# Decayed attention: copying the transposed weights of two heads with one instruction

## The reference, cut to what matters

```
def _L2_attn_ref(x, Wq, bq, Wk, bk, Wv, bv, Wo, bo, alpha):
    q = (x @ Wq.T + bq).reshape(B, T, H, hd)
    k = (x @ Wk.T + bk).reshape(B, T, H, hd)
    v = (x @ Wv.T + bv).reshape(B, T, H, hd)
    scores = jnp.einsum('bqhd,bkhd->bhqk', q, k) * scale
    lag = jnp.abs(idx[:, None] - idx[None, :]).astype(jnp.float32)
    scores = scores * jnp.exp(-alpha * lag * DT)
    attn = jax.nn.softmax(scores, axis=-1)
    out = jnp.einsum('bhqk,bkhd->bqhd', attn, v).reshape(B, T, D)
    return out @ Wo.T + bo
```

## Time and profile before

| what | value |
|---|---|
| median of 3 runs | 4465.07 us |
| lowest and highest run | 4442.44 and 4473.7 us |
| the profiled execution, its own time | 4474.3 us |
| its span in the trace | 4472.5 us |
| decayed attention in it | about 2574 to 3191 us |
| mean granted TensorE clock | 0.822 |

### The profile page before, as it was taken

The page is one execution under the profiler, slowest core; times in us unless marked ns, Lnnn a source line. Parts: engine busy times, 40 slices in busy tenths (PEclk is TensorE's granted clock), DMA queues, the critical chain, the costliest instruction groups (busy, mean ns, idle before and its releaser), DMA issues. The chain is left out here.

```text
span 4472.5 us, 65620 instructions
## 1 busy us (share of the span) xinstructions
PE 3023.8 (68%) x22266; PEld 2082.8 (47%) x22266; DVE 2326.8 (52%) x5222; ACT 1525.0 (34%) x2598; POOL 813.9 (18%) x800
## 2 busy tenths in 40 slices
PE   6999526999932314794346299999881537599990
PEld 4555414777720313442145145555571325476790
DVE  5555663111145463499553488888534468412443
ACT  4444112333322000000222188888531332243340
POOL 0000000000018301200134350000025564000015
PEclk9999757999956556897678599999995768699995
DMA  2000000000000022000034110000151000000471
GB/s 102 1 1 0 1 8 10 5 9 9 5 6 29 6 38 39 1 0 0 4 102 145 37 39 1 1 1 1 55 181 37 31 7 1 11 10 4 140 213 60
DMA packets 124861, 150.88 MB, mean 34 GB/s; under 512 B 50012, under 2 KB 95593, under 8 KB 124041
## 3 DMA queue, kind: packets, MB, share of 16 engines
q1 hardware_dynamic: 106584, 107.60, 8.7%
q0 software_dynamic: 18096, 41.06, 2.9%
HBM read 108.23 MB, written 40.37 MB: 33 GB/s over the span
## 5 line engine op out<-in xcount | busy, mean ns | idle before, releaser
L2183 DVE CUSTOM_DVE_ANT_0 decayed_sd<-decayed_sc,decayed_decay 128x512 f32<-128x512 f32 x512 | 331.7, 686 | 86.2 <-PE decayed_sc L2060 86.0
L2138 ACT ACTIVATE decayed_pr<-decayed_sd,decayed_shift 128x512 f32<-128x512 f32 x512 | 338.9, 713 | 49.5 <-DVE decayed_shift L2190 49.3
L668 PEld LDWEIGHTS experts_down<-experts_w,experts_h 128*128 128x128 f32 x2048 | 263.9, 192 | 107.1 <-issue 103.5
L2072 PEld LDWEIGHTS decayed_tr<-all_ident,decayed_pr 128*128 128x128 f32 x2048 | 223.5, 141 | 175.5 <-ACT decayed_pr L2138 101.7
L2072 PE MATMUL decayed_tr<-all_ident,decayed_pr 128*128 128x128 f32 x2048 | 276.9, 278 | 11.0 <-ACT decayed_pt L2145 10.8
L736 DVE SCALAR_TENSOR_TENSOR L0c_G<-experts_down,all_gate,L0c_G 128x128 f32 x256 | 85.5, 351 | 371.1 <-PE experts_down L668 371.1
L441 PE MATMUL experts_up<-experts_xt,experts_w 128*128 128x256 f32 x1140 | 272.0, 386 | 0.0
L702 ACT ACTIVATE experts_h<-experts_up,experts_w 128x512 f32<-128x512 f32 x256 | 175.9, 687 | 281.1 <-PE experts_up L657 279.7
L668 PE MATMUL experts_down<-experts_w,experts_h 128*128 128x128 f32 x2048 | 264.7, 275 | 0.0
L657 PE MATMUL experts_up<-all_XNT,experts_w 128*128 x512 | 258.7, 597 | 5.3 <-DMA experts_w<-in_L_experts 5.3
L198 PE MATMUL norm_turned<-all_ident,norm_xn 128*128 128x128 f32 x128 | 35.7, 434 | 299.6 <-DVE norm_xn L136 299.6
(11 more groups left out here) (468 smaller groups left out, 6377.1 us busy)
## 6 DMA issues: line engine op xcount, KB each, us to landing
experts_w<-in_L_experts SPq DMA_DIRECT2D x78, 384.0 KB, 3.4
experts_w<-in_L_experts SPq DMA_DIRECT2D x43, 579.0 KB, 4.0
experts_tok<-rows_in SPq DMA_DIRECT2D x121, 128.0 KB, 3.4
rows_out<-experts_y POOLq DMA_DIRECT2D x121, 128.0 KB, 3.4
rows_in<-linear_zero SPq DMA_DIRECT2D x43, 128.0 KB, 1.8
experts_w<-in_L_experts SPq DMA_DIRECT2D x8, 514.0 KB, 3.4
experts_b<-in_L_experts_b SPq DMA_DIRECT2D x43, 64.0 KB, 4.2
moe_w<-in_L_moe SPq DMA_DIRECT2D x4, 514.0 KB, 3.5
```

The source lines that it names most:

```text
L668: last = pe.matmul(down[b % 2][:, t * P:(t + 1) * P], h[:, b % 2, f, t * P:(t + 1) * P], w2, start=(f == 0 and t == 0), stop=(f == nf - 1) ...
L2072: last = pe.transpose(tr[u % TURNED][:, t * P:(t + 1) * P], pr[:, u % RING, t * P:(t + 1) * P], m.ident[:, :])
L2138: act.activation(pr[:, u % RING, :], sd[:, u % RING, :], ACT.Exp, bias=shift[:, u % RING:u % RING + 1]).then_inc(exp_ready, 1)
L2183: dve.tensor_tensor_reduce(out=sd[:, u % RING, :], in0=sc[h][:, :], in1=decay[:, qt, :], scale=1.0, scalar=-3.0e38, op0=ALU.mult, op1=ALU. ...
```

## The change

The two `tr` banks become one tensor `[P, 2, 512]`, so that one instruction can read both. `keep(g, h)` now copies heads `h` and `h + 1` at once, 1024 columns. ScalarE runs it once a quad for heads 0 and 1, VectorE once a quad for heads 2 and 3. A copy waits until both of its heads are transposed (`g * G + h + 2`). The semaphores `act_kept` and `dve_kept` count one for each quad in place of two. TensorE waits before head 0 for VectorE's copy of the quad before, and before head 2 for ScalarE's copy of heads 0 and 1; heads 1 and 3 have no wait on a copy any more. On VectorE `negate(g, 1)` stands ahead of the copy.

```diff
-        sc, tr, proj, av = s.banks("sc", G), s.banks("tr", TURNED), s.banks("proj", 1)[0], s.banks("av", 1)[0]
+        sc, proj, av = s.banks("sc", G), s.banks("proj", 1)[0], s.banks("av", 1)[0]
+        tr = s.enter_context(nc.psum_tensor(f"{phase}_tr", [P, TURNED, 512], F32))
...
-            return pt[:, n % 2, :, h, qt * P:(qt + 1) * P], tr[(g * G + h) % TURNED][:, :].rearrange("p (t q) -> p t q", t=TPB)
+            return (pt[:, n % 2, :, h:h + 2, qt * P:(qt + 1) * P].rearrange("p t h q -> p h t q"),
+                    tr[:, :, :].rearrange("p h (t q) -> p h t q", t=TPB))
...
-                if h < 2:
-                    reached(pe, dve_kept, 2 * (g - 1) + h + 1)
-                else:
-                    pe.wait_ge(act_kept, 2 * g + h - 1)
+                if h == 0:
+                    reached(pe, dve_kept, g)
+                if h == 2:
+                    pe.wait_ge(act_kept, g + 1)
                 for t in range(TPB):
-                    last = pe.transpose(tr[u % TURNED][:, t * P:(t + 1) * P], pr[:, u % RING, t * P:(t + 1) * P], m.ident[:, :])
+                    last = pe.transpose(tr[:, u % TURNED, t * P:(t + 1) * P], pr[:, u % RING, t * P:(t + 1) * P], m.ident[:, :])
...
-                    pe.wait_ge(act_kept, 2 * TPB * (n + 1))
-                    pe.wait_ge(dve_kept, 2 * TPB * (n + 1))
+                    pe.wait_ge(act_kept, TPB * (n + 1))
+                    pe.wait_ge(dve_kept, TPB * (n + 1))
...
             def keep(g, h):
-                act.wait_ge(tr_ps, g * G + h + 1)
+                act.wait_ge(tr_ps, g * G + h + 2)
...
                     keep(g - 1, 0)
-                    keep(g - 1, 1)
...
             def keep(g, h):
-                dve.wait_ge(tr_ps, g * G + h + 1)
+                dve.wait_ge(tr_ps, g * G + h + 2)
...
-                if is_quad(g - 1):
-                    keep(g - 1, 2)
                 if is_quad(g):
                     negate(g, 1)
                 if is_quad(g - 1):
-                    keep(g - 1, 3)
+                    keep(g - 1, 2)
```

## The result

The changed kernel took 4529.5 us (median of 4 runs, 4510.8 to 4548.3) against 4454.7 for the kernel before on the same chip (4 runs, 4442.4 to 4473.7): ratio 1.0164, interval 1.0093 to 1.0235. It is slower, by 41 to 105 us. A ratio here is always a kernel's time over that of the kernel before, with a 95% interval. The profiled execution of the changed kernel took 4548.3 us, 74.0 more than that of before.

What follows compares the result with a forecast made beforehand. TensorE was taken to bound the decayed attention stage. Longer steps (38.1 + 26.7 + 10.2 us) and 6.4 us for held-up work made 81 us, on a median of 4465 giving 4546 us, range 4515 to 4585.

Steps and rivals of the forecast that it cites:

- T01 to T23: TensorE, start of heads 0 and 1's transposes to start of heads 2 and 3's: 1.43 to 2.02 us before, 2.35 predicted.
- The wait that is added: TensorE before head 2's transposes: must await ScalarE's copy of heads 0 and 1, 2.35 us after head 0's start, every step.
- the three rows of the sum: Added TensorE time by what precedes head 2: projection 68 steps, 38.1 us; nothing 29, 26.7 us; weighing 31, 10.2 us.
- the last one: TensorE behind heads 2 and 3's transposes: starting out of a wait, they hold the next work longer, 6.4 us in all.
- the row with 1.05: TensorE step with nothing between the transpose groups: 1.05 us from heads 2 and 3's transposes to the next work, after waiting.
- The copies: Merged copies out of PSUM: ScalarE 1.04 us, VectorE 1.21; saves 6 and 10 us of engine time, nothing on the path.
- VectorE's hand-over: TensorE before the next step's head 0: VectorE's pair copy allows it 2.50 us after T23, just hidden; nothing charged.
- The clock: Rival: TensorE's busy share falls to 87%; a tenth of the stage at the lower clock adds 50 us, 4596; chance 0.07.
- The cheaper hand-over: Rival: ScalarE's hand-over to TensorE takes only 2.0 us from T01 to T23, adding 31 us, 4496; chance 0.08.
- Engine time counting after all: Rival: VectorE or ScalarE ends the waits for scores, so saved copy time shortens steps: 4449, or 4431; chance 0.05.
- The bank rule: No two engines on one PSUM bank at once, so a copy over both banks leaves TensorE none to write; unpriced.
- the row with the 0.34 wait: TensorE step with nothing between the transpose groups: 1.43 us from T01 to T23, 0.34 of it waiting for ScalarE's copy.

Runs made afterwards that it cites:

- The move in the kernel before: Kernel before, with the third step's weighing moved from behind the transposes of heads 2 and 3 to ahead of them: ratio 0.9974.
- the waits alone: Kernel before with its 512-column copies kept, but the changed kernel's waits and VectorE order: ratio 1.0161 to the kernel before.
- the changed kernel with the moved weighing: Changed kernel, with the third step's weighing moved from behind the transposes of heads 2 and 3 to ahead of them: ratio 1.0125 to the kernel before.

## Why the prediction was right

- **What bounds the stage.** TensorE's order. The move in the kernel before shows it from one side (idle time taken out of it shortens the stage), the waits alone from the other (T01 to T23 grew by 74 us over all steps, the stage by 76.5).
- **The wait that is added.** Right in place, cause and size: 2.29 us from T01 to T23 in every step against 2.35 predicted. The parts: 1.13 to ScalarE's start (1.16), 1.02 for the copy (1.04), 0.14 to TensorE (0.15).
- **The sum.** 81 us predicted, 68.1 in the stage, so the forecast was 13 too high. With 2.29 the three rows of the sum are 34.0, 24.9 and 8.4, 67.3 in place of 75.0. The term that was mis-sized most is the last one, 6.4 us for work that T23 holds up after a wait: it is 0.90 and 0.99 us from T23 to the next instruction in the covered steps (0.87 and 0.97 before), and 1.00 where 1.05 stood before and was taken for all (2923.35 to 2924.35). So it gives 1.7 us in the 68 steps and takes more than that back in the others (1.5 in the 29 by that row, and 0.02 in each of the 31, where it was 1.02): in all it is nothing. Counted over all steps, T01 to T23 grew by 66.7 us, of which 0.9 are the first step's lower clock, and T23 to the next T01 by 1.5, in the first set and the last. A likely reason for the row with 1.05, not tested: T23 waited twice there, for head 0's copy and for head 1's, and its eight transposes took 1.12 us where they now take 1.06.
- **The copies.** Slopes from other copies out of PSUM gave 1.04 and 1.21 us; measured 1.025 and 1.225. That merging is worth nothing where the engine has idle time holds: VectorE's merge alone changes nothing that can be told.
- **VectorE's hand-over.** Predicted at 2.50 us from T23 to T01 and just hidden. It measured 2.47 in the changed kernel with the moved weighing, and was hidden in the changed kernel but for 4 waits, 1.3 us in all.
- **The clock.** It stayed at 1.00 in the stage but for its first step (a granted clock of 0.51 from 2581 to 2584 us, T01 to T23 3.18 us in place of 2.29). TensorE's busy share fell less than predicted:

```profile
2600.00:3250.00 650.00, 586.13 (x4270) 307.32 (x4274) 509.94 (x1427) 493.42 (x711) 39.65 (x41) 1.00 0.02 5
```

586.1 of 650 us is 90%, against 98% before and 87% predicted. This window of the changed kernel (columns as in the earlier trace rows) holds some us behind the stage's last transposes.
- **The rivals.** The cheaper hand-over (2.0 us) is out by the 2.29. Engine time counting after all is out by VectorE's merge. The Trainium skill (VectorE: DVE Perf Modes, The TRN2 errata) has a large tile pay the fixed cost of an instruction once. The trace agrees in part: 16.4 and 7.0 us less busy time on the two engines, 23 against the 34 estimated from that page. None of it reached the end.
- **The bank rule.** The prediction took the row with the 0.34 wait as a sign that no two engines may be on one bank. It shows only a wait that the kernel's code asks for; no run here puts two engines on one bank at once, and nothing in the sum hangs on it.
- **The range.** Its own terms give 4546 - 6 - 15 = 4525 at the low end, not the 4515 stated. The result lies above both.

The measured median, 4529, is 17 below the 4546 predicted. With its fourth run the median of before is 4455 in place of 4465, which is 10 of them; the medians differ by 75, which is 6 less than 81. That they differ by 75 and not by the stage's 68 comes from stages that the change doesn't touch, so part of the closeness is luck.

## What to carry to other kernels

Merging two copies of a double buffer into one saves a fixed cost once and turns the double buffer into a single one: the producer can no longer fill one half while the other is drained. Price it as a hand-over, from the first write of the pair to the end of its copy and on to the next write, and compare that with the work that the producer has in between; here 2.29 us stood against 0.9 to 2.0 on one side and 2.47 against mostly 2.5 to 3.1 on the other, and nearly all of the cost came from the first. Where a trace shows the producer waiting in some steps of a cycle, see whether work of the same step can stand inside the gap, before touching the copies: moving one weighing gave 0.26%, and no merge gave anything.

## What the runs showed of the hardware

One instruction can read two neighbouring banks at no extra cost that shows: 1024 columns took 1025 ns on ScalarE and 1225 on VectorE, where 512 took 591 and 685, so 0.85 and 1.05 ns for each further column. Within one bank VectorE's rows give 1.02 (425 ns for 256 columns, 685 for 512).

Executions differ by some 35 us in a stage that nobody changed. While an earlier layer runs, GpSimd issues 64 indirect transfers; the same instruction took 1739 ns each in the profiled execution before, 1641 in the changed kernel's, and 1072 in that of the changed kernel with the moved weighing (groups by line from 1230 to 1530 us, of before and of that kernel):

```profile
L367 POOL DMA_INDIRECT rows_in<-L_T,all_slot x64 | 111.3, 1739 | 67.2 <-POOLq L1244 48.0 <-issue 19.2
```

```profile
L367 POOL DMA_INDIRECT rows_in<-L_T,all_slot x64 | 68.6, 1072 | 67.1 <-POOLq L1244 47.9 <-issue 19.2
```

That kernel's decayed attention began at 2546.7 us where the others had 2580 to 2591. The time of the 64 instructions is enough to account for it: 64 x (1739 - 1072) ns is 43 us, and the stage began 41 us earlier than in the kernel before. The edit is not the reason, since runs of one kernel lie on both sides: one of that kernel took 4495 us and four 4535 to 4542, and the changed kernel has 4511 and 4513 beside 4546 and 4548. Only one execution of each was profiled, though, and why the transfers differ was not tried. It is the reason that the lengths of the stage above tell more than the totals.
